# Delta rules on one core: seven gate tiles' products between the Gram products of the front part, their Silu in the merging stage

## The reference, cut to what matters

```python
q = _l2norm(_silu(h @ Wq).reshape(Bs, Ls, H, DK))
k = _l2norm(_silu(h @ Wk).reshape(Bs, Ls, H, DK))
v = _silu(h @ Wv).reshape(Bs, Ls, H, DV)
def step(S, x):
    qt, kt, vt, bt, gt = x
    S = S * jnp.exp(gt)[..., None, None]
    kv = jnp.einsum('bhk,ebhkv->ebhv', kt, S)
    delta = (vt[None] - kv) * bt[..., None]
    S = S + kt[None, :, :, :, None] * delta[..., None, :]
    ot = jnp.einsum('bhk,ebhkv->ebhv', qt * scale, S)
    return (S, ot)
...
core = jnp.einsum('ble,eblhv->blhv', w_full, o)
gate = _silu((h @ Wg).reshape(Bs, Ls, H, DV))
core = core * jax.lax.rsqrt(jnp.mean(core * core, axis=-1, keepdims=True) + 1e-05)
core = core * o_norm_weight * gate
return core.reshape(Bs, Ls, VDIM) @ Wo
```

## Time and profile before

| | |
|---|---|
| median of 3 runs | 3242.42 us (3235.12 to 3244.03) |
| span of the profiled execution, first to last instruction | 3179.3 us |
| own time of the profiled execution | not listed apart; the median lies 63.1 us above its span |
| PE busy in the span | 2868.6 us (90%) |
| DVE, ACT, POOL busy | 1667.8, 1138.0, 1497.0 us |
| front part of `delta` | from 1340 to about 1427 us of the span |
| last chains | from about 1791 to 1930 us |
| `merge` | from 1932 us |

### The profile page before, as it was taken

One profiled execution on the slowest core, in us unless ns is written; L12 is line 12 of the kernel. 1 busy time (PEld: TensorE's weight loads), 2 busy tenths in 40 slices (PEclk: granted clock), 3 DMA queues, 4 the chain that ended last, 5 costly groups with the idle time before them and its releaser, 6 DMA issues.

```text
span 3179.3 us, 46211 instructions
## 1 busy us (share of the span) xinstructions
PE 2868.6 (90%) x16081; PEld 1650.9 (52%) x16081; DVE 1667.8 (52%) x3712; ACT 1138.0 (36%) x2501; POOL 1497.0 (47%) x1471
## 2 busy tenths in 40 slices
PE   6999999988899989958999998999999999999828
PEld 3433566667667644437777764444533333444324
DVE  7633356578444442256777643442368888521361
ACT  3312422279222222345666542220045454331201
POOL 0565755578645538642333204544666666200004
PEclk9999999999999989988999999999999999999859
DMA  5400001120111224434445555211176676500504
GB/s 175 142 19 5 7 23 48 52 71 16 33 45 46 75 99 161 180 90 129 133 129 150 141 144 163 82 60 37 42 221 213 204 214 199 146 0 27 185 0 133
DMA packets 275816, 320.84 MB, mean 101 GB/s; under 512 B 155791, under 2 KB 193553, under 8 KB 275588
## 3 DMA queue, kind: packets, MB, share of 16 engines
q1 hardware_dynamic: 219540, 182.05, 18.6%
q0 software_dynamic: 51840, 134.60, 13.8%
q10 hardware_dynamic: 4208, 1.25, 0.2%
HBM read 215.22 MB, written 104.60 MB: 101 GB/s over the span
## 4 chain that ended last, share of the span: by engine, by line
PE 80%; DVE 7%; ACT 6%; issue 5%; DMA 2%; POOL 1%; SPq 0%; DVEq 0%; ACTq 0%; POOLq 0%
PE bank L1522 5%; PE bank L2737 5%; PE bank L708 4%; PE bank L2728 4%; PE bank L1301 4%; PE bank L2393 3%; PE bank L2909 3%; PE bank L2902 3%; PE bank L439 3%; PE bank L2137 2%; PE bank L731 2%; PE bank L2150 2%; PE bank L762 2%; PE bank L1117 2%; PE bank L2128 2%
## 5 line engine op out<-in xcount | busy, mean ns | idle before, releaser
L2708 POOL DMA_INDIRECT conv_src<-xn_rows,keep x288 | 290.4, 1009 | 140.8 <-issue 95.9
L291 POOL DMA_INDIRECT sorted_bias<-perf_rec,place x256 | 259.2, 1013 | 146.5 <-PE bank L708 92.1
L2737 PE MATMUL bank<-conv_msg,conv_hot 128*128 128x512 f32 x432 | 203.5, 594 | 0.0
L666 POOL DMA_INDIRECT sorted_edge<-rec,place x128 | 126.8, 990 | 141.7 <-PE bank L1362 75.2
L1933 POOL TENSOR_TENSOR delta_dec<-delta_dec,rates_of 128x512 f32<-128x512 f32 x64 | 66.5, 1039 | 253.3 <-ACT delta_dec L1985 253.3
L2788 DVE TENSOR_TENSOR conv_msg<-bank,conv_src 128x1024 f32<-128x1024 f32 x144 | 175.7, 1220 | 18.0 <-PE bank L2728 18.0
L1117 PE MATMUL bank<-bias_prod,bias_hot 128*128 128x256 f32 x640 | 148.2, 387 | 25.3 <-ACT bias_hot L1070 13.1
L2728 PE MATMUL bank<-conv_we,conv_eT 64*128 64x512 f32 x576 | 165.5, 652 | 1.1 <-ACT conv_eT L2762 1.1
L1101 POOL TENSOR_TENSOR bias_prod<-bias_col,bias_rec 128x512 f32<-128x512 f32 x128 | 147.2, 1179 | 16.6 <-PE bank L1117 15.8
L1117 PEld LDWEIGHTS bank<-bias_prod,bias_hot 128*128 128x128 f32 x640 | 120.2, 192 | 53.8 <-issue 28.2
L2766 ACT ACTIVATE conv_msg<-conv_msg 128x1024 f32<-128x1024 f32 x108 | 114.2, 1057 | 87.3 <-DVE conv_msg L2788 87.3
(11 more groups left out here) (508 smaller groups left out, 6794.2 us busy)
## 6 DMA issues: line engine op xcount, KB each, us to landing
keep<-slot_qkv SPq DMA_DIRECT2D x32, 512.0 KB, 4.7
delta_kv<-slot_qkv SPq DMA_DIRECT2D x32, 512.0 KB, 3.9
sorted_edge<-sort_pad SPq DMA_DIRECT2D x8, 1440.0 KB, 7.6
keep<-sorted_edge SPq DMA_DIRECT2D x18, 640.0 KB, 5.4
slot_out<-delta_o SPq DMA_DIRECT2D x64, 128.0 KB, 2.7
conv_src<-xn_rows,keep POOLq DMA_INDIRECT x288, 3.7
X<-in_x SPq DMA_DIRECT2D x4, 1024.0 KB, 11.1
sorted_bias<-perf_rec,place POOLq DMA_INDIRECT x256
```

The source lines that it names most:

```text
L291: POOL.indirect_dma_start(out=sorted_bias, out_offset=bass.IndirectOffsetOnAxis(ap=place[:, 0, c:c + 1], axis=0), in_=rec0[:, c, :], in_of ...
L2708: POOL.indirect_dma_start(out=src[:, n % 4, j, :], out_offset=None, in_=xn_rows, in_offset=bass.IndirectOffsetOnAxis(ap=rec[:, g % 3, k + ...
L2737: a = PE.matmul(bank[n % 2][:, :], hot[:, g % 2, k + j, :].bitcast(F32), msg[:, q, j, :], start=j == 0, stop=j == 1)
```

## The change

The seven tiles' products leave the last chains and stand in the front part, at positions 9.65 to 13.25, all in bank 3 (which nothing uses before `Z` of unit 0). Since it is one bank, each tile waits until ACT has copied the one before. ACT's copy is a plain one now (no Silu), into two spare slots of `more_kq`; the raw product goes to `gate_rows`. In `merge`, ACT applies Silu in place to the loaded rows, once per tile. Wg and the seven tiles of the input are loaded at positions 1.9 to 1.96 into memory of `BA` and `kv` that is not yet in use; Wg is loaded a second time for the four late tiles, as before.

```diff
+            FIRST_GATES = NT - EARLY_GATES - LATE_GATES
+            gate_at = (9.65, 10.65, 11.65, 11.74, 12.65, 12.74, 13.25)
+            held_at = (9.75, 10.75, 11.72, 11.8, 12.72, 12.8, 13.36)
             plan.append((NC - 0.6, "gate weights", 0))
-            for t in range(NT - EARLY_GATES):
-                plan.append((max(NC + 0.4, after_all + each * (t - 2.2)), "gate in", t))
-            for t in range(NT - EARLY_GATES - LATE_GATES):
-                for c in range(KC):
-                    plan.append((after_all + each * (t + c / KC), "gate", (t, c)))
-                plan.append((after_all + each * (t + 1.3), "gate out", t))
+            for t in range(LATE_GATES):
+                plan.append((NC + 0.4, "gate in", t))
+            for t in range(FIRST_GATES):
+                plan.append((1.9 + 0.01 * t, "first gate in", t))
+                plan.append((gate_at[t], "gate", t))
+                plan.append((held_at[t], "gate out", t))
...
+                    if what == "first gate in":
+                        if n == 0:
+                            SP.dma_start(first_wg, rows(I["L0_ffn_Wg"])).then_inc(*first_wg_in.up(16))
+                        SP.dma_start(first_gate_rows(n), xnT_tiles[EARLY_GATES + n]).then_inc(*xg_in[n % 4].up(16))
...
                     if what == "gate out":
                         ACT.wait_ge(*gate_done.at(n + 1))
                         if n >= 2:
                             ACT.wait_ge(*gate_out[n % 2].at(16 * (n // 2)))
-                        else:
-                            ACT.wait_ge(*BA_ready.at(NC))
-                        ACT.activation(flat4(dec[:, n % 2, :, :]), bank[1 + n % 2], AF.Silu).then_inc(*gate_active.up())
+                        ACT.activation(first_out[:, n % 2, :], bank[3], AF.Copy).then_inc(*gate_active.up())
...
                     if what == "gate":
+                        if n == 0:
+                            PE.wait_ge(*first_wg_in.at(16))
+                        else:
+                            PE.wait_ge(*gate_active.at(n))
+                        PE.wait_ge(*xg_in[n % 4].at(16 * (n // 4 + 1)))
+                        for c in range(KC):
+                            a = PE.matmul(bank[3], first_gate_rows(n)[:, c * P:(c + 1) * P], first_wg[:, c, :], start=c == 0,
+                                          stop=c == KC - 1)
+                        a.then_inc(*gate_done.up())
...
+            plan += [(t - 1.3, "gate", t) for t in range(EARLY_GATES, NT - LATE_GATES)]
...
-                        if t < NT - LATE_GATES:
+                        if t < EARLY_GATES:
                             POOL.wait_ge(*gate_in[q].at(16 * (t // 4 + 1)))
+                        elif t < NT - LATE_GATES:
+                            POOL.wait_ge(*gate_ready.at(t - EARLY_GATES + 1))
...
+                    if what == "gate":
+                        ACT.wait_ge(*gate_in[q].at(16 * (t // 4 + 1)))
+                        ACT.activation(gate_of(t), gate_of(t), AF.Silu).then_inc(*gate_ready.up())
```

More of the change, by code:

```diff
@@ L1831, in gate_rows_in @@
             def gate_rows_in(t):
-                return xg[:, t % 2, :] if t % 4 < 2 else qk[:, 2, t % 2, :]
+                return xg[:, t, :] if t < 2 else qk[:, 2, t - 2, :]
             plan.sort(key=lambda x: x[0])
@@ L1970, in scalar @@
                             ACT.wait_ge(*through.at(n - 2 * R + 1))
+                        elif n == 2 * (R - 1):
+                            for g_ in range(2):
+                                ACT.wait_ge(*gate_out[g_].now())
                         ACT.activation(kq(t)[:, 2 * g:2 * g + 2, :, :], turn_bank(n).rearrange("p (i k n) -> p i k n", i=2, k=2),
@@ L2098, in tensor @@
                             PE.wait_ge(*Z_ready.at(n))
+                        else:
+                            PE.wait_ge(*gate_active.at(FIRST_GATES))
                         for i, h in enumerate(heads):
@@ L2190, in vector @@
                             DVE.wait_ge(*attended.at(n - 2 * R + 1))
+                        elif n == 2 * (R - 2):
+                            DVE.wait_ge(*gate_done.at(FIRST_GATES))
                         for e in range(2):
@@ L2278, in program @@
                     plan.append((t + at, what, t))
+            plan.sort(key=lambda x: x[0])
+            plan += [(t - 1.3, "gate", t) for t in range(EARLY_GATES, NT - LATE_GATES)]
             plan.sort(key=lambda x: x[0])
```

35 lines of the change are left out of this document (15 added, 20 removed).

## The result

The changed kernel takes 3288.68 us (median of 4 runs, 3283.34 to 3292.72) against 3239.47 for the kernel before (4 runs, 3235.12 to 3244.03): ratio 1.0141, 95% interval 1.0114 to 1.0169. I had forecast 3236 with a range to 3249. It came out on the side to which I gave 0.09.

The account below looks back on a forecast made before the run. Last chains bound by PE's order while gate products stand there, then by PE-ACT-PE-DVE latency; front part by DVE's block chain. Terms -15.1 + 5.0 + 1.0 + 2.5 = -6.6 from 3242.4 give 3236, range 3226 to 3249.

Parts of the forecast that it names:

- Term 1: Last chains: without gate products most steps drop to 5.95 us, a gain of 15.1 us, range 11 to 19.
- step 53 with its `L copy`: Last chains: `L copy` stands ahead of the two copies on which `solve` waits, +1.2 us.
- the block chain: Last chains, steps 47 to 50: DVE still does block chain 7, making r late by some 0.4 in each, +1.5 us.
- the 1.0 for "UL in": Last chains: "UL in" feeds `Z` every second step with 5.95 us instead of 6.9 to do it, taken as +1.0.
- the clock falls in the last chains: Last chains: products kept PE busy; slow steps cost 3.2 us each, eight give 3261; chance 0.09, shared with another stall.
- its sign: Last chains' windows in the changed kernel's trace: a clock below 1.00 for more than one stretch.
- Term 2: Front: eight loads ahead of "load qk" 3 make `turn` 6 late, +5.0 us, and slow PE's clock, +1.0.
- Term 3: Front: seven tiles on PE nearly fit its pauses; the last ones delay `decay` 14, +2.5 us, between +1.5 and +5.
- The first rival: Front costs next to nothing: terms 2 and 3 together +2, time 3229; chance 0.32, shared with a larger term 1.
- Term 4: Merge: seven Silus of some 0.6 us fit where ACT is idle, 0; without that cover 4.2 us.

Follow-up runs that it names:

- e6: Changed kernel plus one idle 128x512 product right ahead of `solve` in each of the last eighteen steps; ratio to the kernel before 0.9969.
- e2: Changed kernel with 28 idle products and seven Silu copies put back at the places of the kernel before; ratio to the kernel before 1.0038.
- e8: As e6, with the front's eight loads issued behind "load qk" 3 instead of ahead of it; ratio to the kernel before 0.9959.
- e11: As e8, with three more idle products right ahead of `solve` of step 45; ratio to the kernel before 0.9971.
- e14: As e8, but idle products only in the pauses of steps 46 to 59, steps 60 to 63 bare; ratio to the kernel before 0.9960.
- e3: Changed kernel with only the first eight of the 28 idle products, in steps 46 and 47, without copies; ratio to the kernel before 1.0128.
- e5: Changed kernel with only the first sixteen of the 28 idle products, in steps 46 to 53, without copies; ratio to the kernel before 1.0109.
- e10: As e8, but idle products only in the pauses of steps 46 to 55, steps 56 to 63 bare; ratio to the kernel before 0.9999.
- e13: Kernel before, with each of seven gate tiles' four 512-column products cut to one of 32 columns, loads, Silus and stores kept; ratio 1.0128.

## Why the prediction was wrong, step by step

**Term 1, the last chains: -15.1 forecast, +39.2 measured. This step failed.** The prediction took the clock as given: "12 steps stay, now 1903.86 - 1814.45 = 89.4 us, then 12 x 5.95 = 71.4." The 5.95 was read from four bare steps that followed fourteen full ones. I took them as proof that a bare step runs at full clock. They are proof only that the clock outlasted four of them. What the runs showed in its place is a step of 9.45 us at a granted clock of 0.50. The rest of the sum was sound: with the clock held by a product in each pause, the same stretch takes 113.7 us, 16.1 less than before (e6), against the 15.1 forecast, and step 53 with its `L copy` took 7.18, 1.2 above its neighbours, as the term had it. The excess of steps 47 to 52 was 1.6 us, with 1.5 forecast for the block chain; the 1.0 for "UL in" shows in no step, since steps 54 to 62 take 5.95 or 5.96.

**The rival "the clock falls in the last chains" is what happened.** Its price was near: 3.2 us a slow step forecast, 9.45 - 5.95 = 3.5 measured. But it priced five to eight slow steps, and all eighteen were slow: (169.0 - 114.8) / 3.5 is more than fifteen beyond those that the sum had. And its sign was worded for more than one stretch of low clock, where there was a single one. Its chance, 0.09, rested on the window 1905 to 1925, the same four bare steps. What should have weighed against that window: the low clock behind step 45's stall was in the earlier trace rows, and the change takes away the very products that stood there when the clock came back. No row showed a bare step in which it rose. The Trainium skill (TensorE: Matmul & The Clock Gate, section on HAM oscillation) describes a kernel that loses the fast clock again and again because waits for transfers, some 3 to 5 us each, break up its compute. By that rule the change loses, and it did. The trace agrees only in part: the waits here are of 0.86 us, and the clock didn't come and go but stayed low for 184.3 us.

**Term 2, the loads: +6.0 forecast, 6.6 measured.** The six kernels with the loads early (changed, e2 to e6) have fronts of 117.7 to 120.8 us, mean 119.63; the five with them behind "load qk" 3 (e8 to e11, e14) 111.1 to 114.0, mean 113.07. The mechanism was right as well. The pause ahead of `turn` 6 was 4.08 us, within the 3.8 to 5.9 forecast, and it ended 11.5 us after the first of the eight issues (1380.75), with 11.1 to 13.2 forecast from issue to landing; the DMA engines moved 385 GB/s in 1383 to 1391. The clock fell in this pause, for 6.8 us from 1391.1, and does not fall there in e8. I took 5.0 for the pause and 1.0 for the slow clock; how the 2.5 us beyond the pause split was not taken apart.

**Term 3, the seven tiles on PE: +2.5 forecast, 0.6 measured**, the mean of 113.1 against 112.5 in the four profiles with the old front (113.0, 113.1, 113.2, 110.7), which is nothing that such a spread can show. The inner step was right: without the loads' delay `decay` 14 comes 79.9 us behind the stage's start in e8, against 76.9 before, 3.0 later where 2.6 was forecast. Two of the three were made up again before the first `w` (114.0 against 113.0), although the prediction held that a late front is never made up. From `decay` 14 to 15 alone it is 1.1 us, 3.2 against 4.3 before. In the changed kernel `turn` comes 3.43 us behind the start of a tile at full clock (1409.87 to 1413.30), as forecast. The first rival had the clock right for this stretch: its slow windows behind 1380, 27.3 us of low clock between 1384.2 and 1418.4 before, are gone in e8 and in the changed kernel. The forecast had 1.1 us for that; what it was worth in full was not measured.

**Terms 2 and 3 together: +8.5 forecast, +6.5 measured. Term 4, merging: 0 forecast, 0.9 measured** in one pair of profiles, and 1.3 us more at the head of the stage. e2's 2.5 us behind the last `w` are of the same size; no experiment was made on it, and I leave it at "small".

**Open.** Why four bare steps kept the clock at the end of the kernel before, in both of its profiles and in e2, and one or two lost it in e3, e5, e10 and e14. The busy time of such steps is the same. What precedes differs (in e10 and e14 steps of 5.96 us with one product in the pause, against steps of 7.75 with two outside it), but no run tells whether that is the reason; e3 and e5 had steps with products outside the pause ahead of theirs too (6.87 to 8.11 us) and lost the clock, there with a longer last pause ahead of the fall (1.69 and 1.04 us). Nor is it shown that the pause itself is what counts: steps of 7.75 us have the same pause of 0.86 us and kept the clock at 1.00. A product that a bare step gets outside its pause, or a pause filled with less, was not tried.

## What to carry to other kernels

Before work is taken off TensorE in a stretch bound by latency, look at what stretches of that bare kind do after a stall, not only at how they run behind full ones: here the same step takes 5.95 us at one clock and 9.45 at the other, and once at the second it stayed there to the end of the chains. Filling the pause that every step has cost 0.01 us a step in this kernel with one product and 0.8 with two, so try to move work into the pause before moving it to another stage. And when bulk loads are brought forward, put them behind the next small load that something waits for.

## What the runs showed of the hardware that I had not expected

- For 184 us PE was busy by the profile 0.90 to 0.91 of the time (36.55 of 40 us) at a granted clock of 0.50, and did not get the other half; bare steps that kept 1.00 show it busy 5.03 of 6 us. At 1.2 GHz its own matmuls are longer (1.97 against 1.11 us), so in these runs the busy share didn't tell at which clock PE would go on.
- Taking 28 products (32.0 us of busy time) out of a kernel, with only seven small ones of 32 columns left of them, made it some 41 us slower (e13).
- A 128x512 product of 1.12 us in a pause of 0.86 us cost 0.01 us a step, while two of them outside the pause cost 1.8 (7.75 against 5.95).
